# The dt projection of a Mamba and experts layer contracts over 64 rows instead of 16, the added rows being zero

## The chip, the cores and the metric

The kernel runs on one core of a Trainium2 chip. The metric is the device time of one execution, in microseconds (us), the lower the better. Weights are laid out on the host before the launch; the times are of the launch alone.

## The reference

The input x has 32 batches of 512 tokens of width 256, all float32. One layer is computed: a layer norm, a Mamba block, an MLP, a layer norm, and then a mixture of eight experts of which each token takes two, with one shared expert, and a last layer norm. What matters here is the part of the Mamba block between its projections and its scan:

```python
dbc = xc @ x_proj_w.T                       # 512 channels -> 16 + 16 + 16
dt, Bm, Cm = jnp.split(dbc, [16, 32], axis=-1)
dt = jax.nn.softplus(dt @ dt_proj_w.T + dt_proj_b)   # 16 -> 512 channels
def step(h, inp):                            # over the 512 tokens
    dA = jnp.exp(dt_t[..., None] * A)
    h = dA * h + (dt_t * x_t)[..., None] * B_t[:, None, :]
    y = jnp.einsum('bdn,bn->bd', h, C_t)
```

The dt projection, dt @ dt_proj_w.T, contracts over only 16 values for each token. It is the one matmul that the change touches.

## The kernel before, in words

Channels lie on the 128 partitions, tokens along the free axis, so one batch of the 512 inner channels is four tiles of 128x512. All matmuls on the way are float32; each appears in the profile as two MATMUL records (and two LDWEIGHTS).

Each engine runs one list of instructions whose order is fixed when the kernel is built. It is woven from strands: `scan`, `turn` and `weigh` (the state scans, the transposes of their results, and the sum over states), `pre` (everything that leads to the scan of a batch), `post` (everything behind it), and `inputs`, `experts`, `results`, `finish`. The function `weave` merges the strands by a table of places, in which one batch is 64 ticks long; `pre` of a batch runs at negative places, so beside the scans of the batch before it. The tables are the same in both kernels. In steady state, work of three batches is interleaved: the scans of one, the preparation of the next, and the MLP and routing of the one before. Between two engines there are only semaphores; each `wait_ge` stands in front of one instruction and holds back all that is queued behind it on that engine.

The steady work of a batch b:
- ScalarE makes exp(dt*A) for each of 64 (state, tile) pairs into the two banks `psA` (line 755); GpSimdE multiplies dtx by a spread row of B into `dBx` (line 600); VectorE runs the scan into `hs` (line 1231); TensorE transposes `hs` into the banks `psH` (line 977); VectorE adds the transposed state, weighted by C, into `acc` (line 1247).
- TensorE's `pre` for the next batch: transposes of x (line 933), the input projection (942), then the x projection (950), which contracts 128 rows four times and gives 48 rows of output; ScalarE copies those 48 rows to the tile `dbc` (728); four transposes of its C rows (957); and then the dt projection (966): for each of the four channel tiles j, one matmul of 16 rows, with 128 columns of weights and 512 of tokens. All four, for every batch but the first, write to one PSUM bank, `psP`. ScalarE reads the bank twice, for Abs (738) and Relu (741), and matmul j waits for Relu j-1 (`s_dt_relu`).
- Between those four matmuls TensorE's list holds transposes of the running scans (977) and the z projection of `post` (994).
- The expert pairs (1115, 1133, 1148) and the MLP (1040, 1057) fill other places.

The tile `few`, 128 partitions of 1024 floats, holds several small things one above another. Partitions 0 to 15 of its first 512 columns are `w_dt`, the weights of the dt projection, loaded once. Partitions 0 to 47 of the last 512 columns are `dbc`: 16 rows of dt, 16 of B, 16 of C. Partition 64 has small tables for routing, and partition 96 the bias `b2`. Before the change nothing writes partitions 16 to 63 of the weights' columns, nor partitions 48 to 63 of `dbc`'s.

SyncE's list begins with the loads of the weights (line 385), one after another in a fixed order, `dt_proj_w` sixth. VectorE's list begins with small memsets of tables (1195 to 1200) and then waits for all weights. The functions that the diff touches:

Of the kernel before, what the change touches and what calls it, by code (L numbers as in the profile page):

```python
# [116 lines left out]
def build(nc, a, out):  # L117
# [4 lines left out]
    P = 128  # L122
    NB, T, D = a["x"].shape
    DI = a["conv_w"].shape[1] * P
# [4 lines left out]
    R = a["dt_proj_w"].shape[0]  # L129
# [52 lines left out]
    with ctx:  # L182
        def sb(name, shape, dtype=F32):
            return ctx.enter_context(nc.sbuf_tensor(name, shape, dtype))

        def sem(name):
            return ctx.enter_context(nc.semaphore("s_" + name))
# [52 lines left out]

        few = sb("few", [P, DI + T])
        M0, B2 = 64, 96
        w_dt, dbc = few[0:R, 0:DI], few[0:NX, DI:DI + T]
        b2 = few[B2:B2 + 1, 0:D]
        taken, table = 0, []
        for n in (NE * (CAP // P), NT, NE, NE, NE, NT * NE, NT, NT):
# [54 lines left out]
        s_B_in = [sem(f"B_in{i}") for i in range(NBB)]  # L301

        s_zeroed, s_consts, s_halved, s_A_exp = sem("zeroed"), sem("consts"), sem("halved"), sem("A_exp")

        s_bn_post, s_mean_post = sem("bn_post"), sem("mean_post")
        s_tap, s_scan, s_weighed = sem("tap"), sem("scan"), sem("weighed")
# [39 lines left out]
        def per_batch(b, j, n):  # L346
            return b * n + j + 1
# [23 lines left out]
        def bank(b, j):  # L371

            return psP if b else (psP, psE, psG[0], psG[1])[j]
# [8 lines left out]
        @block.sync  # L382
        def _(sp):
            for dst, key_ in loads:
                sp.dma_start(dst if key_ == "dt_proj_w" else dst[:], a[key_]).then_inc(s_weights, 16)
            sp.dma_start(b2, a["mlp_b2"]).then_inc(s_weights, 16)
            sp.dma_start(w_shared[:], a["experts"][NE]).then_inc(s_weights, 16)
# [528 lines left out]
        def _(pe):  # L916
# [5 lines left out]
            def pre():  # L922
                for b in range(NB):
                    xn, c = xnT[b % 2], xc[b % 2]
                    for k in range(KD):
                        yield b
                        pe.wait_ge(s_norm_pre, (b + 1) * NTB)
                        if k:
                            pe.wait_ge(s_xnT, per_batch(b, k - 1, KD))
                        elif b:  # L930
                            pe.wait_ge(s_dt_relu, b * CT)
                        for t in range(NTB):
                            i = pe.transpose(psP[:, t * P:(t + 1) * P], tok_pre[b % 2][:, t, k * P:(k + 1) * P],
                                             ident[:])
                        i.then_inc(s_xn_turned, 1)
                    for j in range(CT):
                        yield b
                        pe.wait_ge(s_xnT, (b + 1) * KD)
                        if b and j:
                            pe.wait_ge(s_tap, per_batch(b, j - 1, CT) * (NK - 1))  # L940
                        for k in range(KD):
                            i = pe.matmul(bank(b, j)[:], w_in[:, k, j * P:(j + 1) * P], xn[:, k, :], start=(k == 0),  # L942
                                          stop=(k == KD - 1))
                            if k == 0:
                                yield b
                        i.then_inc(s_in_mm, 1)
                    yield b
                    pe.wait_ge(s_silu_x, b + 1)
                    for k in range(CT):
                        i = pe.matmul(psP[0:NX, :], w_x[:, k, :], c[:, k, :], start=(k == 0), stop=(k == CT - 1))  # L950
                        if k < CT - 1:
                            yield b
                    i.then_inc(s_x_mm, 1)
                    yield b
                    pe.wait_ge(s_dbc, b + 1)
                    for t in range(NTB):
                        i = pe.transpose(psP[:, t * NS:(t + 1) * NS], dbc[R + NS:NX, t * P:(t + 1) * P],
                                         ident[R + NS:NX, R + NS:NX])
                    i.then_inc(s_C_turned, 1)
                    for j in range(CT):  # L960
                        yield b
                        if j == 0:
                            pe.wait_ge(s_C_tok, b + 1)
                        elif b:
                            pe.wait_ge(s_dt_relu, per_batch(b, j - 1, CT))
                        pe.matmul(bank(b, j)[:], w_dt[:, j * P:(j + 1) * P], dbc[0:R, :], start=True, stop=True).then_inc(  # L966
                            s_dt_mm, 1)

            def turn():
# [182 lines left out]
            def last():  # L1152

                for s_ in range(NLAST + 2):
                    for q, step in ((s_ - 2, 2), (s_ - 1, 1), (s_, 0)):
# [27 lines left out]
                        else:  # L1183
# [4 lines left out]
                            i.then_inc(s_down_last, 1)  # L1188

            weave((turn(), AT["PE_turn"]), (pre(), AT["PE_pre"]), (post(), AT["PE_post"]), (inputs(), AT["PE_inputs"]),  # L1190
                  (experts(), AT["PE_experts"]), (results(), AT["PE_results"]), (last(), AT["PE_last"]))

        @block.vector
        def _(dve):
            dve.memset(where[0], 0).then_inc(s_consts, 1)
            dve.memset(where[1], 0).then_inc(s_consts, 1)
            for k in range(CAP // P):
# [279 lines left out]
```

## Time and profile before

| what | us |
|---|---|
| median of 3 runs | 5192.72 |
| lowest and highest | 5188.47, 5199.28 |
| the profiled execution, its own time | 5198.2 |
| span of the profile | 5196.5 |
| busy: VectorE, TensorE, GpSimdE, ScalarE | 4352.5, 4253.3, 3589.0, 3527.3 |
| mean granted TensorE clock | 0.912 of full |

A busy share is an average over the whole span. The granted clock of TensorE is given as a share of its full speed, 2.4 GHz; the records know only the two values 1.00 and 0.50 (1.2 GHz), and a stretch that holds some of both shows a number between. The batches are counted from 0; batch 10 means the stretch that begins with its first dt matmul.

### The profile page before, as it was taken

The numbers are of one execution on the slowest core, as the hardware profiler recorded it, in microseconds if no ns is written. First come the engines' busy times: TensorE is split into PE (matmuls) and PEld (weight loads), VectorE is DVE, ScalarE is ACT, GpSimd is POOL, SyncE is SP. The second block draws the span as 40 slices with busy tenths as digits, with TensorE's granted clock in tenths as the row PEclk, the third lists the DMA queues.
The fourth block names the chain that finished last, engine by engine and source line by source line (L and its number), as shares of the span: only waits on it lengthen the run. The fifth ranks groups of instructions, "written<-read, shape, count | busy, mean of one in ns | idle before, by whom it ended". The sixth has DMA issues, their size and how long they took to land. (4 is left out here: it accounts for less than half of the span.)

```text
span 5196.5 us, 75832 instructions
## 1 busy us (share of the span) xinstructions
PE 4253.3 (82%) x20928; PEld 2925.9 (56%) x20928; DVE 4352.5 (84%) x6184; ACT 3527.3 (68%) x6433; POOL 3589.0 (69%) x2252
## 2 busy tenths in 40 slices
PE   3788888788888888888888888888888888988882
PEld 2455555565555556555555655555565656655662
DVE  4889899888898898889889888988888888888741
ACT  4666666677766667776776777777677676776642
POOL 4666666666666567777777777777787776787754
PEclk7889899899999999999999999999999889998986
DMA  5122222243333333333333333333344442554555
GB/s 136 54 80 84 84 84 76 74 134 125 112 115 121 108 93 111 100 99 96 96 92 86 105 114 96 96 98 92 84 136 115 121 125 86 165 148 131 161 148 156
DMA packets 357157, 563.53 MB, mean 108 GB/s; under 512 B 40434, under 2 KB 203379, under 8 KB 356611
## 3 DMA queue, kind: packets, MB, share of 16 engines
q1 hardware_dynamic: 286082, 457.85, 28.9%
q0 software_dynamic: 49152, 67.27, 6.3%
q10 hardware_dynamic: 21504, 33.56, 1.7%
q8 instruction: 174, 2.85, 0.2%
q14 instruction: 245, 2.00, 0.1%
HBM read 440.66 MB, written 186.05 MB: 121 GB/s over the span
## 5 line engine op out<-in xcount | busy, mean ns | idle before, releaser
L600 POOL TENSOR_TENSOR dBx<-dtx,Bbc 128x1024 f32<-128x1024 f32 x1024 | 2451.4, 2418 | 684.1 <-DVE hs L1231 632.4
L1231 DVE TENSOR_TENSOR_SCAN hs<-ps,dBx 128x512 f32<-128x512 f32 x2048 | 2409.9, 1207 | 267.9 <-ACT ps L755 91.5
L755 ACT ACTIVATE ps<-dt,A 128x512 f32<-128x512 f32 x2048 | 1393.6, 690 | 610.3 <-DVE hs L1231 596.3
L977 PE MATMUL ps<-ident,hs 128*128 128x128 f32 x8192 | 1323.7, 297 | 461.7 <-DVE acc L1247 296.1
L977 PEld LDWEIGHTS ps<-ident,hs 128*128 128x128 f32 x8192 | 1007.6, 151 | 1018.1 <-DVE acc L1247 519.0
L1247 DVE SCALAR_TENSOR_TENSOR acc<-ps,C_tok,acc 128x512 f32<-128x512 f32 x1792 | 1281.4, 736 | 213.6 <-PE ps L977 193.2
L657 POOL DMA_INDIRECT fx<-Y_slots,slots x256 | 405.5, 1584 | 133.3 <-issue 55.3
L633 POOL DMA_INDIRECT X_slots<-xs,slots x256 | 254.8, 995 | 320.6 <-DVE slots L1358 254.1
L942 PE MATMUL ps<-xnT,w_in 128*128 128x512 f32 x512 | 298.5, 701 | 55.2 <-DVE xc L1220 54.2
L1133 PE MATMUL ps<-xsT,wx 128*128 128x128 f32 x2432 | 322.6, 281 | 23.7 <-ACT xsT L845 23.6
L994 PE MATMUL ps<-xnT,w_in 128*128 128x512 f32 x512 | 340.8, 764 | 0.0
L1133 PEld LDWEIGHTS ps<-xsT,wx 128*128 128x128 f32 x2432 | 301.1, 196 | 41.7 <-issue 40.4
L1220 DVE SCALAR_TENSOR_TENSOR xc<-ps,conv_w,xc 128x511 f32<-128x511 f32 (+2 forms) x384 | 285.3, 744 | 44.5 <-ACT xc L719 36.0
L1040 PE MATMUL ps<-mT,w_m 128*128 128x512 f32 x512 | 239.3, 600 | 26.3 <-ACT mT L801 20.6
L584 POOL TENSOR_TENSOR dt<-dt,dtx 128x1024 f32<-128x1024 f32 x64 | 152.5, 2383 | 141.0 <-ACT dtx L746 141.0
L1024 PE MATMUL ps<-w_out,xc 128*128 128x256 f32 x1024 | 248.0, 379 | 0.0
L1057 PE MATMUL ps<-w_m,post_tmp 128*128 128x256 f32 x1024 | 246.8, 379 | 0.0
L966 PE MATMUL ps<-few 16*128 16x512 f32 x256 | 180.3, 792 | 51.7 <-ACT dt L741 51.4
L719 ACT ACTIVATE xc<-ps,conv_b,conv_w 128x512 f32<-128x512 f32 x128 | 99.3, 776 | 176.8 <-PE ps L942 174.3
L861 ACT ACTIVATE xin<-ps,xin 128x256 f32<-128x256 f32 x304 | 133.0, 468 | 109.7 <-PE ps L1148 109.7
L1057 PEld LDWEIGHTS ps<-w_m,post_tmp 128*128 128x128 f32 x1024 | 191.7, 190 | 25.3
L1024 PEld LDWEIGHTS ps<-w_out,xc 128*128 128x128 f32 x1024 | 191.7, 190 | 24.5
(209 smaller groups left out, 6023.4 us busy)
## 6 DMA issues: line engine op xcount, KB each, us to landing
Bbc<-B_scratch SPq DMA_DIRECT2D x512, 256.0 KB, 3.7
wx<-in_experts SPq DMA_DIRECT2D x308, 384.0 KB, 3.9
Y_slots<-zeros SPq DMA_DIRECT2D x228, 256.0 KB, 4.4
xin<-X_slots SPq DMA_DIRECT2D x308, 128.5 KB, 3.3
Y_slots<-xin SPq DMA_DIRECT2D x308, 128.0 KB, 1.7
xt<-in_x SPq DMA_DIRECT2D x32, 512.0 KB, 4.0
shared<-xt ACTq DMA_DIRECT2D x32, 512.0 KB, 2.6
fx<-shared SPq DMA_DIRECT2D x32, 512.0 KB, 3.6
```

The source lines that it names most:

```text
L600: pool.tensor_tensor(dBx[u % 3][:], dtx[b % 2][:, 2 * h:2 * h + 2, :], Bbc[g % NBB][:, n % CH:n % CH + 1, :].broadcast_to([P, 2, T]), ALU. ...
L657: pool.indirect_dma_start(out=fx[:, t, :], out_offset=None, in_=Y_slots[g % 2], in_offset=bass.IndirectOffsetOnAxis(ap=slots[:, f % NKEPT, ...
L755: act.activation(psA[s % 2][:], dt[b % 2][:, j, :], ACT.Exp, scale=A[:, j, n:n + 1]).then_inc(s_dA, 1)
L942: i = pe.matmul(bank(b, j)[:], w_in[:, k, j * P:(j + 1) * P], xn[:, k, :], start=(k == 0), stop=(k == KD - 1))
L977: i = pe.transpose(psH[w % 2][:, j * P:(j + 1) * P], hs[(n * CT + j) % NHB][:, t * P:(t + 1) * P], ident[:])
L994: i = pe.matmul(psG[j % 2][:], w_in[:, k, DI + j * P:DI + (j + 1) * P], xn[:, k, :], start=(k == 0), stop=(k == KD - 1))
L1024: i = pe.matmul(psG[q][:, t * D:(t + 1) * D], c[:, k, (2 * q + t) * P:(2 * q + t + 1) * P], w_out[:, k, :], start=False, stop=(k == CT - 1))
L1057: i = pe.matmul(psG[q][:, t * D:(t + 1) * D], post_tmp[:, k, (2 * q + t) * P:(2 * q + t + 1) * P], w_m2[:, k, :], start=False, stop=(k == ...
L1133: i = pe.matmul(psE[:, o * HALF + m * P:o * HALF + (m + 1) * P], w[:, m, (2 * k + o) * P:(2 * k + o + 1) * P], xsT[:, (m * KD + k) * P:(m ...
L1220: dve.scalar_tensor_tensor(out=c[:, j, s:], in0=bank(b, j)[:, 0:T - s], scalar=conv_w[:, j, NK - 1 - s:NK - s], in1=c[:, j, s:], op0=ALU.m ...
L1231: dve.tensor_tensor_scan(hs[s % NHB][:], psA[s % 2][:], dBx[s // 2 % 3][:, s % 2, :], 0.0, ALU.mult, ALU.add).then_inc(s_scan, 1)
L1247: dve.scalar_tensor_tensor(out=o, in0=psH[w % 2][:], scalar=C_tok[b % 2][:, t, n:n + 1], in1=o, op0=ALU.mult, op1=ALU.add).then_inc(s_weig ...
```

## The change

The dt projection reads 64 partitions of `few` on both sides instead of 16. Of the weights, rows 16 to 63 are zero, so the B and C rows that now stream through the array beside dt are multiplied by zero, and so are the 16 rows below them, which are zero too. For this, one VectorE memset at the very start clears partitions 0 to 63 of the whole tile `few`, and the load of `dt_proj_w` on SyncE waits for it by a new semaphore.

```diff
         w_dt, dbc = few[0:R, 0:DI], few[0:NX, DI:DI + T]
+        M_DT = 64
+        w_dt0, dbc0 = few[0:M_DT, 0:DI], few[0:M_DT, DI:DI + T]
...
+        s_few = sem("few")
...
             for dst, key_ in loads:
+                if key_ == "dt_proj_w":
+                    sp.wait_ge(s_few, 1)
                 sp.dma_start(dst if key_ == "dt_proj_w" else dst[:], a[key_]).then_inc(s_weights, 16)
...
-                        pe.matmul(bank(b, j)[:], w_dt[:, j * P:(j + 1) * P], dbc[0:R, :], start=True, stop=True).then_inc(
+                        pe.matmul(bank(b, j)[:], w_dt0[:, j * P:(j + 1) * P], dbc0, start=True, stop=True).then_inc(
                             s_dt_mm, 1)
...
         def _(dve):
+            dve.memset(few[0:M_DT, :], 0.0).then_inc(s_few, 1)
             dve.memset(where[0], 0).then_inc(s_consts, 1)
```

## Rows read from the trace of the kernel before

**Rows 1.** Page: busy time by engine, and granted clock in 40 slices.

```profile
PE 4253.3 (82%) x20928; PEld 2925.9 (56%) x20928; DVE 4352.5 (84%) x6184; ACT 3527.3 (68%) x6433; POOL 3589.0 (69%) x2252
PEclk7889899899999999999999999999999889998986
```

**Rows 2.** Windows, one batch each: stretch, length, busy time by engine, clock, DMA share.

```profile
1489.70:1639.90 150.20, 129.95 (x655) 89.22 (x654) 133.63 (x187) 104.25 (x181) 97.48 (x58) 0.94 0.37 120
3313.30:3463.00 149.70, 126.97 (x657) 86.86 (x655) 133.38 (x187) 109.56 (x201) 112.04 (x70) 0.97 0.35 101
1040.30:1189.30 149.00, 126.33 (x655) 86.95 (x654) 133.36 (x187) 104.50 (x182) 97.36 (x58) 0.97 0.42 132
```

**Rows 3.** Waits: engine, tile and line, whom it waited for, us, times, longest.

```profile
DVE acc L1247 <- PE ps L977: 193.2, 201, 2.9
```

**Rows 4.** One line each: instructions, duration in ns (min/median/max), first and last start.

```profile
L966 PE MATMUL ps<-few x256: 587/692/1217, 50.6 to 4785.0; 16*128 16x512 f32 x128
L942 PE MATMUL ps<-xnT,w_in x512: 592/592/1223, 27.5 to 4751.2; 128*128 128x512 f32 x171
```

**Rows 5.** Timeline of PE, batch 10, dt projection: start, us, instruction, idle before it.

```profile
1489.72 1.12 PE L966 MATMUL ps<-few 16*128 16x512 f32 x2
1492.19 2.07 PE L966 MATMUL ps<-few 16*128 16x512 f32 x2 [1.36 <-ACT dt L741]
...
1498.65 1.18 PE L966 MATMUL ps<-few 16*128 16x512 f32 x2
1499.76 1.13 PE L994 MATMUL ps<-xnT,w_in 128*128 128x512 f32 x2
1501.18 1.12 PE L966 MATMUL ps<-few 16*128 16x512 f32 x2 [0.30 <-ACT dt L741]
...
1503.14 1.92 PE L994 MATMUL ps<-xnT,w_in 128*128 128x512 f32 x2
```

**Rows 6.** Timeline of PE, batch 22, the same instructions.

```profile
3321.93 1.12 PE L966 MATMUL ps<-few 16*128 16x512 f32 x2
3322.99 1.13 PE L994 MATMUL ps<-xnT,w_in 128*128 128x512 f32 x2
3324.41 1.12 PE L966 MATMUL ps<-few 16*128 16x512 f32 x2 [0.30 <-ACT dt L741]
...
3325.95 1.02 PE L994 MATMUL ps<-xnT,w_in 128*128 128x512 f32 x2
```

**Rows 7.** Windows of 20 us from the first dt matmul, batches 10 and 22.

```profile
1489.70:1509.70 20.00, 17.58 (x52) 8.93 (x52) 15.84 (x19) 13.06 (x20) 11.54 (x6) 0.74 0.31 107
3313.30:3333.30 20.00, 17.59 (x69) 9.50 (x68) 17.84 (x21) 14.94 (x22) 12.07 (x6) 0.83 0.32 98
```

**Rows 8.** Windows late in the dt projection, batches 2, 31, 22.

```profile
327.90:331.90 4.00, 4.00 (x13) 2.09 (x12) 1.88 (x2) 2.39 (x5) 1.40 (x1) 0.57 0.17 54
4784.90:4788.90 4.00, 4.00 (x13) 2.23 (x12) 1.88 (x2) 2.93 (x6) 3.69 (x3) 0.62 1.06 275
3325.20:3329.20 4.00, 3.95 (x21) 2.33 (x20) 3.04 (x4) 3.15 (x6) 1.36 (x1) 1.00 0.21 50
```

**Rows 9.** Windows with the clock full: x projection (48 columns), and a thinner stretch.

```profile
1632.00:1637.60 5.60, 4.77 (x16) 1.44 (x14) 5.60 (x7) 4.19 (x7) 4.79 (x4) 1.00 0.28 97
1605.10:1610.10 5.00, 3.43 (x24) 2.75 (x24) 4.97 (x7) 4.84 (x10) 3.88 (x3) 1.00 0.01 2
```

**Rows 10.** Windows late in batches 7 and 8.

```profile
1165.30:1170.30 5.00, 3.12 (x6) 1.16 (x7) 3.73 (x13) 0.00 (x0) 0.00 (x0) 0.74 0.94 294
1309.30:1314.30 5.00, 5.00 (x22) 3.26 (x21) 4.90 (x10) 3.33 (x7) 3.83 (x2) 0.68 0.00 0
```

**Rows 11.** Timeline of the start, all engines.

```profile
1.27 0.54 POOL L547 MEMSET xin<- 128x514 f32 x1
...
3.15 0.43 SPq L385 DMA_DIRECT2D few<-in_dt_proj_w  x1
...
13.80 0.29 DVE L1202 TENSOR_SCALAR w_shared<-w_shared 128x256 f32<-128x256 f32 x1 [10.15 <-DMA w_shared<-in_experts]
```

## The prediction

> **What bounds the kernel now.** I read the page first: VectorE is busy 84% of the span and TensorE 82%, and the clock row shows TensorE below full clock somewhere in nearly every slice [rows 1]. Neither engine is full, so the question is who waits for whom, and where. One batch as a window gives 150.2 us, 133.6 of them with VectorE busy [rows 2]: 16.6 us of a batch is all that a faster TensorE could ever give, and most of that belongs to other engines and places. The list of waits names the place that matters here: VectorE's weighted sum (line 1247) waits 193.2 us in all for TensorE's transposes (line 977) [rows 3].
>
> The timeline of TensorE around the dt projection shows when that happens. In batch 10 the first dt pair takes 1.12 us, the second 2.07 [rows 5]; at full clock a pair of 512 columns takes 1.02 us (the z projection in [rows 6]). So the clock has fallen to 1.2 GHz right behind the first dt matmul. It comes back by the third (1.18), and falls again right behind the fourth: the z projection that starts at 1503.14 takes 1.92 us. What the engine did before that second fall is telling. From 1498.65 to 1503.1 it was never idle for more than 0.30 us, yet two of its three 512-column matmuls there were the dt matmuls of 16 rows [rows 5]. Elsewhere the clock stays at 1.00 over a thinner stretch, 3.43 us busy of 5.0, that has no 16-row matmul in it, and also over one of 4.77 us of 5.6 in which the x projection does most of the work, with 48 columns of weights but all 128 rows [rows 9]. Busy time alone doesn't tell these apart and the weights' columns don't either; the rows that stream do.
>
> The two falls differ in what they cost. Batch 22 has the first fall but not the second (its z projection at 3325.95 takes 1.02 us [rows 6]). Over 20 us from the first dt matmul, batch 10 has 15.84 us of VectorE work and a clock of 0.74, batch 22 has 17.84 and 0.83 [rows 7]: VectorE's list is the same there, so the second fall costs VectorE 2.0 us.
>
> **The change part by part.**
>
> *The matmul itself.* 128 dt matmuls (256 records) with 64 rows instead of 16. The trace has none of 64 rows; the nearest rows on both sides are 16 rows, 587 ns at least and 692 in the median, and 128 rows, 592 ns in both [rows 4]. The rows don't change how long 512 columns stream; the 100 ns between the median of the one and the other go, at most, if it no longer pays what a 16-row matmul pays behind a 128-row one: 256 x 0.1 = 26 us of TensorE's time won at best, and as much lost if 64 rows paid double. Neither lies on the path, since VectorE and ScalarE set the pace there. I take 0.
>
> *The second fall.* It stands behind the fourth dt matmul in 21 of the 32 batches: batches 2, 4, 8 to 15, 17 to 19, 21, 23 to 28 and 31, of which [rows 8] shows the first, the last, and one without it (0.57 and 0.62 against 1.00, VectorE 1.88 against 3.04 us of 4.0). Before it the array is busy nearly without a gap, so four times the rows in two of three matmuls should keep the clock. How much of the 2.0 us lasts to the end of the batch can be read from batches that lack the fall: batch 7 takes 149.0 and batch 22 149.7 us, against 150.2 for batch 10 [rows 2], so 1.2 and 0.5 us are kept. The rest is given back at the end of the batch, where another fall meets the input projection: batch 7 has 0.74 and VectorE busy only 3.73 of 5.0 us there, while in batch 8 it comes 6 us earlier, in a stretch where VectorE loses nothing (4.90 of 5.0) [rows 10]. I take 1.2, batch 7's, as its expert work is the same as batch 10's. 21 x 1.2 = 25 us; with 0.5 it would be 10, with all of the 2.0, 42.
>
> *The first fall.* All 32 batches have it, from about 1492 to 1498.6 in batch 10, some 7 us. In front of it TensorE does one dt matmul, a few transposes and then waits 1.36 us for Relu [rows 5]. More rows can't fill that idle time. Even in batch 22, which has this fall alone, VectorE is idle only 20 - 17.84 = 2.16 us in the 20 [rows 7]; if the first fall went too, up to 32 x 2.16 = 69 us would follow. I take 0 here, because idle time stands in front of the fall, and keep 69 as the far end.
>
> *The start.* The memset of 64x1024 is bounded by GpSimdE's 128x514 in 0.54 us: about twice that, 1.1 us [rows 11]. SyncE reaches the load of `dt_proj_w` at 3.15 us, and VectorE's next work after its tables waits until 13.80 for the last weights. So the new wait finds the semaphore already set, with eleven loads queued behind it that would otherwise slip; and VectorE's 1.1 us lies under 10.15 us of idle time. 0; without that cover 1.1 us once.
>
> Sum: 0 - 25 + 0 + 0. Against the profiled execution's own 5198.2 us that is 5173; this execution lay 5.5 above the median of 5192.7, so 5168.
>
> **The rivals.**
>
> *No change (5193).* The clock would heed only whether TensorE is busy, and 16 rows would be as good as 128. For it: a fall also stands behind idle time, as in the first fall, and the second one could be its echo, since TensorE has just come back from 1.2 GHz. Against it: the nearly gapless stretch in front of the second fall beside the thinner one that keeps its clock [rows 5, 9]. It also covers the case that rows with zero weights don't count. The Trainium skill, "TensorE: Matmul & The Clock Gate", Part 1, says that the clock gate is set "based on how busy the PE has been recently" and says nothing of rows; by that rule this kernel's time would stay at 5193, and [rows 9] against [rows 5] speak against it.
>
> *Both falls go (5130).* If 64 rows count enough to carry even the thin stretch, TensorE arrives at the third dt matmul some 3 us earlier, half of the 7 us spent at half the clock. Priced at half of the far end above, 35 us, on top of the 25: 5133, and some luck at the end of the batch makes 5130. For it: the stretch ahead holds transposes of 128 rows beside the dt matmul. Against: 1.36 us idle.
>
> *Slower (5212).* The order of work is fixed, and where a fall lands depends on when the batch arrives. A batch shorter by 1 or 2 us shifts all later falls; if the shift holds the late one steadily in the input projection, where it takes 5.0 - 3.73 = 1.27 us from VectorE in batch 7 [rows 10], and an additional one in that place takes as much again, 30 batches lose 2.5 us each = 76, less the full local gain of 21 x 2.0 = 42 and the part of the loss that batches already pay, some 15: about 19 us slower. It decides if less than 1.3 us of the local gain is left over per batch. Against it: batches 7 and 22 had exactly this and were still shorter.
>
> **How the numbers follow.** Forecast 0.58, no change 0.18, both falls 0.16, slower 0.08. The forecast's own range goes from 5150 (all of the 2.0 kept) to 5185. The whole range takes in both falls at 5115 (nearly the far end of 69 us) and, above, no change: 5115 to 5193. What a measurement can tell from no change is about 0.2%, 10 us. Within the forecast, about one part in eight lies inside that. Faster: 0.51 + 0.16 + a little of the rest = 0.70; same: 0.07 + 0.15 = 0.22; slower 0.08.
>
> **What would show it.** Right: in the profile of the changed kernel the clock over the first 20 us of batches 8 to 15 is 0.83 or more instead of 0.74 and VectorE has about 17.8 us of work there; the z projection behind the fourth dt matmul takes 1.02 us; the mean clock rises from 0.912 to about 0.925; VectorE's wait for line 977 drops from 193 us by some 30 to 40; batches last 149 us. The dt records themselves stay at 587 to 692 ns. Wrong: the fourth dt matmul is still followed by a pair of 1.92 us (then rows don't count, or not enough), or the falls go and the batches still last 150.2 us, which would mean that the gain is given back before the batch ends.

## The result

The changed kernel takes 5133.1 us (median of 4 runs, 5114.8 to 5143.9) against 5190.6 us of the kernel before, run beside it. The ratio is 0.988, 95% interval 0.985 to 0.992. That is 57 us faster, where 25 were forecast. It lies inside the whole range (5115 to 5193) but outside the forecast's own, 5150 to 5185, and at the time of the rival "both falls go" (5130). Repeated on two different chips, it gave 0.988 (0.986 to 0.990) and 0.990 (0.987 to 0.992). The profiled execution took 5135.8 us with a span of 5134.1 and a mean granted clock of 0.930 (0.912 before). The added lines shift the numbers: line 385 is now 390, 741 is 746, 966 is 971, 977 is 982, 994 is 999, 1231 is 1237, 1247 is 1253; in the experiments an added matmul shifts them by one or two more.

The page of the changed kernel, the lines that answer to [rows 1]:

```profile
PE 4166.5 (81%) x20928; PEld 2875.0 (56%) x20928; DVE 4350.4 (85%) x6185; ACT 3522.6 (69%) x6433; POOL 3586.6 (70%) x2252
PEclk6999999899999999999999999999999899999986
```

VectorE's work is what it was (4352.5 before). TensorE's busy time fell by 87 us though it streams the same columns: it is the same work at a higher clock. From the list of waits, how long VectorE's weighted sum waits for TensorE's transposes; it was 193.2 us in [rows 3]:

```profile
DVE acc L1253 <- PE ps L982: 155.5, 188, 2.9
```

The dt matmul itself, answering to [rows 4] (duration in ns, min/median/max): 587/692/1217 became

```profile
L971 PE MATMUL ps<-few x256: 589/693/1219, 50.7 to 4724.4; 64*128 64x512 f32 x128
```

So 64 rows take as long as 16 did, to within 2 ns. Over 20 us from the first dt matmul, batches 10 and 14 of the changed kernel (length, busy time of PE, PEld, DVE, ACT and POOL, clock, DMA share and GB/s), for [rows 7]:

```profile
1474.70:1494.70 20.00, 17.58 (x66) 9.49 (x66) 17.23 (x20) 14.85 (x22) 11.80 (x5) 0.83 0.32 108
2073.30:2093.30 20.00, 16.48 (x79) 9.28 (x78) 19.48 (x23) 16.82 (x24) 12.22 (x7) 1.00 0.36 116
```

The two lines are the two main kinds of batch that the changed kernel has. Batch 10 has lost the second fall and kept the first, and looks as batch 22 did before: 0.83, and 17.23 us of VectorE's work, against 0.74 and 15.84 in batch 10 before. Batch 14 has lost both: over these 20 us the clock is at 1.00 throughout, and VectorE is busy 19.48 of 20 us. TensorE's timeline in batch 10, for [rows 5]:

```profile
1477.14 1.98 PE L971 MATMUL ps<-few 64*128 64x512 f32 x2 [1.36 <-ACT dt L746]
1479.06 1.97 PE L982 MATMUL ps<-ident,hs 128*128 128x128 f32 x8
1480.82 1.91 PE L999 MATMUL ps<-xnT,w_in 128*128 128x512 f32 x2
...
1484.84 1.12 PE L999 MATMUL ps<-xnT,w_in 128*128 128x512 f32 x2
1486.26 1.12 PE L971 MATMUL ps<-few 64*128 64x512 f32 x2 [0.30 <-ACT dt L746]
...
1487.81 1.02 PE L999 MATMUL ps<-xnT,w_in 128*128 128x512 f32 x2
```

The second dt pair still takes 1.98 us and the transposes and the z projection behind it 1.97 and 1.91, so the first fall is there. The z projection behind the fourth dt matmul, 1.92 us in [rows 5], takes 1.02 at 1487.81. The same work in batch 14, with the idle time in front of the second dt matmul unchanged at 1.36 us:

```profile
2073.32 1.12 PE L971 MATMUL ps<-few 64*128 64x512 f32 x2
2075.80 1.12 PE L971 MATMUL ps<-few 64*128 64x512 f32 x2 [1.36 <-ACT dt L746]
2076.86 1.09 PE L982 MATMUL ps<-ident,hs 128*128 128x128 f32 x8
2077.78 1.02 PE L999 MATMUL ps<-xnT,w_in 128*128 128x512 f32 x2
```

All at 2.4 GHz: 1.12, 1.09 and 1.02 us.

I counted the falls in the profiles, over batches 1 to 31. A batch has the first fall if the clock is at 1.2 GHz for more than 1 us between its first and third dt matmul, and the second if it is for more than 1 us between 9.6 and 16.5 us from the first (batches 16 and 20 of the kernel before have a longer first fall and no second).

| kernel | first fall, of 31 | second fall | us at 1.2 GHz in the whole profile |
|---|---|---|---|
| before, 16 rows | 31 | 21 | 921 |
| changed, 64 rows, profiled three times | 17, 20, 17 | 2, 2, 0 | 720, 705, 720 |

The two batches under second fall in the first two profiles, 26 and 28, have one fall there instead of two (in batch 26 it begins 9.0 us in), and the count has them among those that lost the first. So the second fall is gone as forecast, and by this count the first went too in 11 to 14 of 31 batches, which was not.

The count ends 16.5 us into the batch, and the falls behind it changed as well. In the kernel before, each of the 18 batches from 7 to 29 that has the second fall has a third, 20 to 37 us in; in the changed kernel batch 10 has lost it, while batch 14 has one at a new place. Stretches from 25 to 35 us behind the first dt matmul, batch 10 before, batch 10 changed, batch 14 changed:

```profile
1514.70:1524.70 10.00, 7.94 (x32) 4.58 (x31) 8.42 (x11) 8.17 (x20) 9.71 (x5) 0.83 0.25 79
```

```profile
1499.70:1509.70 10.00, 6.61 (x35) 4.42 (x36) 9.70 (x14) 8.44 (x18) 9.79 (x6) 1.00 0.28 91
2098.30:2108.30 10.00, 9.18 (x37) 5.58 (x38) 9.65 (x12) 8.21 (x15) 9.92 (x6) 0.83 0.40 119
```

Batch 14's new fall costs VectorE next to nothing there (9.65 us of work against 9.70).

Whole batches, for [rows 2] (batches 10, 13 and 19):

```profile
1474.70:1624.90 150.20, 128.15 (x656) 88.04 (x655) 133.70 (x187) 103.98 (x182) 97.51 (x57) 0.95 0.38 120
1926.20:2073.30 147.10, 124.47 (x655) 85.66 (x654) 133.04 (x187) 109.72 (x202) 111.86 (x69) 0.99 0.39 113
2823.20:2969.90 146.70, 124.46 (x655) 85.55 (x654) 132.93 (x187) 109.95 (x202) 111.77 (x69) 0.99 0.40 113
```

Batch 10 lasts 150.2 us, exactly as before, though its second fall is gone. Batches 13 and 19 had both falls and lasted 153.0 and 153.1 us; without either they last 147.1 and 146.7.

### The profile page after: what moved, and what is told of

Its sections match the earlier page's. It is cut to its first block and busy times, and to the rows that moved or that the text cites. A ratio compares the mean times of both kernels' runs of the same rounds, so it can differ in the third digit from the quotient of the medians.

```text
span 5134.1 us, 75833 instructions
## 1 busy us (share of the span) xinstructions
PE 4166.5 (81%) x20928; PEld 2875.0 (56%) x20928; DVE 4350.4 (85%) x6185; ACT 3522.6 (69%) x6433; POOL 3586.6 (70%) x2252
## 5 line engine op out<-in xcount | busy, mean ns | idle before, releaser
L982 PE MATMUL ps<-ident,hs 128*128 128x128 f32 x8192 | 1295.6, 292 | 486.6 <-DVE acc L1253 284.5
L982 PEld LDWEIGHTS ps<-ident,hs 128*128 128x128 f32 x8192 | 975.9, 148 | 1013.9 <-DVE acc L1253 527.5
L947 PE MATMUL ps<-xnT,w_in 128*128 128x512 f32 x512 | 292.5, 688 | 57.3 <-DVE xc L1226 56.1
L999 PE MATMUL ps<-xnT,w_in 128*128 128x512 f32 x512 | 299.8, 679 | 0.0
L589 POOL TENSOR_TENSOR dt<-dt,dtx 128x1024 f32<-128x1024 f32 x64 | 153.0, 2391 | 132.2 <-ACT dtx L751 132.2
L971 PE MATMUL ps<-few 64*128 64x512 f32 x256 | 163.5, 724 | 51.1 <-ACT dt L746 50.7
```

The costliest lines, as they stand in the source:

```text
L982: i = pe.transpose(psH[w % 2][:, j * P:(j + 1) * P], hs[(n * CT + j) % NHB][:, t * P:(t + 1) * P], ident[:])
L999: i = pe.matmul(psG[j % 2][:], w_in[:, k, DI + j * P:DI + (j + 1) * P], xn[:, k, :], start=(k == 0), stop=(k == KD - 1))
```

## The experiments

All times are medians beside runs of the kernel before on the same chip, three jobs in all; the kernel before had 5192.4, 5198.8 and 5196.6 us in them. The theory was that the clock of TensorE follows the rows that stream through the array and not its busy time alone (A). The main rival was that rows don't matter and the change only moved the work against the falls, or that busy time is all that counts (B).

**The memset and the wait alone, 16 rows.**

```diff
-        M_DT = 64
+        M_DT = 16
```

(The diff here and in the two runs after it is against the changed kernel; the memset still clears 64 rows.) 

> The changed kernel's memset and wait at the start are kept, but the dt matmul reads 16 rows as before. Theory A: no gain, 5185 to 5200 us, the second fall of the clock back in about 21 of 32 batches. Rival B (the new start shifts the whole program against the clock's falls): 5115 to 5145 us, as with 64 rows.

Measured: 5194.2 us, ratio 1.000 (0.998 to 1.001). First fall in 31 batches, second in 21. Batch 10 over the 20 us:

```profile
1488.00:1508.00 20.00, 17.58 (x52) 8.94 (x52) 15.80 (x19) 13.06 (x20) 11.51 (x6) 0.74 0.30 107
```

The line is that of the kernel before (0.74, 15.80 against 15.84). The start of the program and its new semaphore cost nothing and gain nothing. That part of B is out.

**32 and 48 rows.** The cut is that of 32 rows; the other run has 48 in its place.

```diff
-        M_DT = 64
+        M_DT = 32
```

> 32 rows in the dt matmul, the rest as in the changed kernel. Theory A1 (each row counts): the busy stretch of the third and fourth dt matmul keeps its clock, the thin one of the first two doesn't: 5155 to 5175 us, first fall in all 32 batches, second in none or few. Theory A2 (rows count in groups of 32, of which 16 rows fill one already): no gain, 5185 to 5200 us. If 32 rows do all that 64 do: 5130 us.

> 48 rows, which are exactly the rows that hold data (dt, B and C); no row of zeros streams. Theory A1 (each row counts): between 32 and 64 rows, 5140 to 5170 us; the first fall, which 64 rows take away in 13 of 32 batches, stays in more of them. Theory A2 (groups of 32, two of them filled): the same as 64 rows, 5115 to 5145 us.

Measured: 32 rows 5163.4 us, ratio 0.995 (0.994 to 0.997); 48 rows 5156.1 us, 0.994 (0.991 to 0.996). In the same job the changed kernel itself:

> The changed kernel again, 64 rows, for a firm number beside the others. Theory A (the clock heeds how many rows stream through the array, so the dt matmuls now hold it up): 5115 to 5145 us. Rival B (the gain came from something else, such as where the falls of the clock happened to land): the same, this run doesn't tell them apart.

Measured: 5128.7 us, 0.988 (0.986 to 0.990).

| rows in the dt matmul | us | first fall | second fall | us at 1.2 GHz |
|---|---|---|---|---|
| 16 | 5194.2 | 31 | 21 | 891 |
| 32 | 5163.4 | 31 | 6 | 787 |
| 48 | 5156.1 | 31 | 0 | 757 |
| 64 | 5128.7 | 20 | 2 | 705 |

32 rows, batches 10 and 14 over 20 us, the one without and the other with the second fall:

```profile
1487.70:1507.70 20.00, 17.58 (x66) 9.56 (x66) 17.40 (x20) 14.56 (x21) 12.02 (x6) 0.83 0.30 109
2088.70:2108.70 20.00, 17.59 (x52) 8.79 (x52) 15.92 (x19) 13.12 (x20) 11.64 (x6) 0.74 0.27 95
```

48 rows, batch 10:

```profile
1491.50:1511.50 20.00, 17.58 (x65) 9.52 (x65) 17.26 (x20) 14.89 (x22) 11.80 (x5) 0.83 0.33 108
```

The ladder settles three things. 32 rows already do more than 16, so rows don't count in full groups of 32 (A2 is out for this step). The second fall goes between 16 and 48 rows, the first only between 48 and 64, and in part. (With the second goes the third: of batches 7 to 29, 18 have it with 16 rows and none with 48.) And the step from 48 to 64 adds nothing but zeros, in the weights and in the data, and yet brings 27 us: for the clock, rows of zeros do.

**More busy time, no more rows.** Each dt matmul of the kernel before is issued twice.

```diff
+                        pe.matmul(bank(b, j)[:], w_dt[:, j * P:(j + 1) * P], dbc[0:R, :], start=True, stop=True)
                         pe.matmul(bank(b, j)[:], w_dt[:, j * P:(j + 1) * P], dbc[0:R, :], start=True, stop=True).then_inc(
                             s_dt_mm, 1)
```

> The kernel before, with each dt matmul of 16 rows issued twice into the same bank (the second one's result stands): TensorE is busier by 0.86 us at each of the four places, without more rows at a time. Theory A (rows that stream count): both falls of the clock stay, in 31 and some 15 to 25 batches, and the time is 5190 to 5215 us. Rival B (busy time counts, rows don't): the falls go as with 64 rows and more, 5120 to 5160 us.

Measured: 5423.5 us, ratio 1.043 (1.040 to 1.045). TensorE's timeline of batch 9, lines 966 and 967 being the two dt matmuls:

```profile
1412.63 2.07 PE L966 MATMUL ps<-few 16*128 16x512 f32 x2 [1.36 <-ACT dt L741]
1414.50 1.91 PE L967 MATMUL ps<-few 16*128 16x512 f32 x2
1416.34 1.97 PE L978 MATMUL ps<-ident,hs 128*128 128x128 f32 x8
...
1420.80 2.07 PE L966 MATMUL ps<-few 16*128 16x512 f32 x2
1422.66 1.91 PE L967 MATMUL ps<-few 16*128 16x512 f32 x2
1424.50 2.08 PE L995 MATMUL ps<-xnT,w_in 128*128 128x512 f32 x2
1426.51 2.07 PE L966 MATMUL ps<-few 16*128 16x512 f32 x2
1428.38 1.91 PE L967 MATMUL ps<-few 16*128 16x512 f32 x2
...
1432.83 1.91 PE L978 MATMUL ps<-ident,hs 128*128 128x128 f32 x8
...
1437.29 1.02 PE L995 MATMUL ps<-xnT,w_in 128*128 128x512 f32 x2
```

From 1414.50 to the end of the dt matmuls the timeline shows no idle time of TensorE, and every pair of dt takes 1.9 to 2.1 us, so the clock stays at 1.2 GHz. It is back at 2.4 only behind some 6 us in which nothing but matmuls of 128 rows streamed (1.02 us at 1437.29). The 20 us from the first dt matmul:

```profile
1410.30:1430.30 20.00, 18.64 (x32) 7.20 (x31) 9.66 (x11) 8.72 (x14) 8.97 (x4) 0.53 0.31 108
```

0.53, and VectorE has 9.66 us of work in 20. The expectation was right in the sign and far too low in the price: 225 us more than the kernel before beside it (5198.8), where 5215, 16 more, was the most expected. I had priced the falls as if they kept their length; they grew: in batch 9 the clock is at 1.2 GHz for 24 us without a break. Nor had I priced the added matmuls. All dt matmuls together keep TensorE busy for 387 us instead of 180, much of it at half the clock and in a place where the engine has no idle time; how much of the 225 us is theirs and how much comes from the longer falls, no run separates. Rival B, that busy time is what counts, is out.

**One added matmul in front of the first dt matmul.** The first fall stays in 17 to 20 batches. If rows are what the stretch in front of it lacks, a matmul of 128 rows there should help.

```diff
+                        if j == 0:
+                            pe.matmul(psP[:, 0:256], ident[:], xn[:, 0, 0:256], start=True, stop=True)
                         pe.matmul(bank(b, j)[:], w_dt0[:, j * P:(j + 1) * P], dbc0, start=True, stop=True).then_inc(
```

> The changed kernel (64 rows) with one more matmul in front of the first dt matmul of each batch: identity by 256 columns of the normed input, 128 rows, into the bank that the dt matmul then overwrites, 0.43 us at full clock. Theory A: this is what the thin stretch lacks in the 17 to 20 batches where the first fall stays; it then stays in under 8, and the time is 5085 to 5120 us. If the first fall is worth nothing where it stays: 5129 us and up to 14 more (32 times 0.43).

Measured: 5119.9 us, ratio 0.985 (0.982 to 0.987). First fall in 14 batches, 624 us at 1.2 GHz. Its timeline in batch 10, where the changed kernel had the fall (line 972 is the added matmul):

```profile
1478.56 0.60 PE L972 MATMUL ps<-xnT,ident 128*128 128x256 f32 x2
1479.09 1.12 PE L973 MATMUL ps<-few 64*128 64x512 f32 x2
1481.56 1.12 PE L973 MATMUL ps<-few 64*128 64x512 f32 x2 [1.36 <-ACT dt L746]
...
1483.55 1.02 PE L1001 MATMUL ps<-xnT,w_in 128*128 128x512 f32 x2
```

Repeated on another chip:

> 64 rows with the added matmul of 128 rows and 256 columns in front of the first dt matmul, again. If its lead over the changed kernel is real, a ratio of about 0.985 to the kernel before (5115 to 5125 us); if it was the draw of that job, 0.988.

> The changed kernel (64 rows) once more, on the same chip as the three variants that go beyond it. 5115 to 5145 us, a ratio of 0.988 to the kernel before.

Measured: 5116.7 us, 0.985 (0.983 to 0.987), against 5135.3 us, 0.990 (0.987 to 0.992), for the changed kernel on the same chip. So the added matmul, useless as arithmetic, wins another 19 us. The intervals of the ratios just touch, but each of its six runs (5107.5 to 5120.3) is faster than each of the six of the changed kernel (5122.6 to 5157.6), and the first job gave the same 0.985. This is the fastest version that was run. It removed fewer falls than expected (14 and 13 left, not under 8), but it halved most that it left: 13 of the 14 and 11 of the 13 last about half as long as the usual first fall, of the changed kernel's 17 to 20 only 2 to 4. In the first 9.6 us of batches 1 to 31 the clock is at 1.2 GHz for 53 and 55 us in sum, against 114 to 124 in the changed kernel. This, more than the count, goes with the 19 us.

The same added matmul with 16 rows:

```diff
+                        if j == 0:
+                            pe.matmul(psP[:, 0:256], w_dt[:, 0:P], dbc[0:R, 0:256], start=True, stop=True)
```

> As the run before, but the added matmul has 16 rows instead of 128: the same 0.43 us of TensorE, an eighth of the rows. Theory A: the first fall stays in 15 to 22 batches as without it, 5125 to 5145 us. Rival B (busy time counts): the same as with the added matmul of 128 rows.

Measured: 5168.3 us, 0.994 (0.991 to 0.996). First fall in 28 of 31 batches. Batch 10 over 20 us with 16 rows in the added matmul, and then with 128:

```profile
1506.80:1526.80 20.00, 17.59 (x67) 9.55 (x66) 16.94 (x20) 14.72 (x21) 11.82 (x5) 0.83 0.33 110
```

```profile
1479.10:1499.10 20.00, 16.44 (x79) 9.26 (x78) 19.04 (x23) 16.86 (x24) 12.03 (x6) 1.00 0.38 135
```

0.83 against 1.00, and 16.94 against 19.04 us of VectorE's work, for nearly the same time on TensorE (0.69 us the pair with 16 rows, 0.60 with 128): 48 us between the two kernels. It gains 31 us over the kernel before beside it, where 64 rows with nothing added gain 57 to 64 in the other jobs: it is 27 to 33 us slower than those, where at most 16 were expected. The 16-row matmul doesn't only fail to help, it also brings falls that weren't there; why was not tried further.

The added matmul without the change:

> The kernel before (16 rows) with the added matmul of 128 rows and 256 columns in front of the first dt matmul of each batch. Theory A: the first fall goes in some 5 to 12 of the batches, the second stays in 15 or more: 5165 to 5190 us. If what the added matmul does were independent of the dt matmul's rows, it would gain here what it gains over the kernel with 64 rows.

Measured: 5195.5 us, 0.999 (0.998 to 1.000); first fall in 25 batches, second in 19. Some falls went, as expected (850 us at 1.2 GHz against 891 with 16 rows in the ladder), but the time didn't follow: 5165 to 5190 us were expected. Where it was lost was not traced; that the added matmul costs as much as it gains is not shown. Together with the 64 rows it is worth more than alone.

More of the same:

> As fill64 with 512 columns in the added matmul, 0.86 us instead of 0.43. Theory A: the first fall, left in 14 of 31 batches by 256 columns, is left in 5 or fewer; each is worth at most some 2 us and the longer matmul costs 0.43 us in each batch that didn't need it, so 5105 to 5130 us. If the falls that are left don't depend on what stands in front of the first dt matmul, still about 14 of them and 5120 to 5140 us.

> As fill64, with the same added matmul also in front of the second dt matmul of each batch but the first. It stands behind the wait for Relu, so behind the idle time. If the falls that 256 columns leave begin only behind the second dt matmul, they go too: 5 or fewer batches with the first fall, 5100 to 5125 us. If they are set before it, the second added matmul only costs: 5120 to 5140 us, as many falls as fill64.

The first puts 512 columns into the added matmul; the second adds one also in front of the second dt matmul:

```diff
-                        if j == 0:
+                        if j < 2 and (b or j == 0):
```

Measured: 5136.9 us, 0.989 (0.986 to 0.992), and 5131.5 us, 0.988 (0.985 to 0.991). First falls 19 and 20. Both expectations on the falls were wrong: no fewer were left than with one matmul of 256 columns. Batch 14, without falls there, with the longer matmul, over 20 us:

```profile
2076.10:2096.10 20.00, 16.41 (x79) 9.23 (x78) 18.61 (x22) 16.89 (x24) 11.82 (x6) 1.00 0.36 117
```

VectorE has 18.61 us of work in it where the shorter one left 19.04 (batch 10 above; both numbers recur to 0.1 us in the other batches from 9 to 24 whose clock is full over the 20 us, and with nothing added it is 19.4 to 19.5). So each 0.43 us of added matmul takes 0.43 us from VectorE here. Why falls remain that this doesn't reach is open. In the batches that keep them they mostly begin elsewhere, 3.3 to 4.5 us behind the first dt matmul, where batches 8 to 11 of the changed kernel have 1.8 to 2.6; I ran nothing that holds that place fixed.

## Why the prediction was right, and where its sizes were off

**In short.** The mechanism held: more rows keep the clock, and the second fall goes. The sum did not: 25 us were forecast and 57 to 64 measured, because the first fall, a term taken at 0, also went in part, and because the second was priced too low. That the time still lies in the range is owed to the far end kept for "both falls go", to which 0.16 was given; the forecast's own 5150 to 5185 missed it.

**What bounds the kernel** held. That VectorE idles in this place because TensorE's low clock makes its transposes late is shown by VectorE's 19.48 us of work in 20 as soon as the clock is full.

**The matmul's own time**, taken as 0: right, 589/693 ns against 587/692.

**The start**, taken as 0: right, both by the run with 16 rows and by its rows, where the memset ends at 2.00 (it takes 0.91 us, 1.1 were estimated) and SyncE comes to the load at 3.18, 3.15 before:

```profile
1.09 0.91 DVE L1200 MEMSET few<- 64x1024 f32 x1 [1.09 <-PEq L1474]
...
3.18 0.43 SPq L390 DMA_DIRECT2D few<-in_dt_proj_w  x1
```

**The second fall** was the one that was priced, at 21 x 1.2 = 25 us. The mechanism is shown: it is gone with 48 rows, which leave the first fall in all 31 batches, so that kernel measures this term, with the third fall that goes with it: 5194.2 - 5156.1 = 38 us, 1.8 for each of 21. The local price of 2.0 us was too high, as batch 22 is not batch 10: in batch 10 itself VectorE wins 1.4 us over the 20 (15.84 to 17.23). The share that lasts was too low. But it isn't a share of each batch. In batch 10 nothing was kept: over its last 40 us, kernel before and then changed,

```profile
1599.70:1639.90 40.20, 32.14 (x164) 20.85 (x162) 38.60 (x75) 24.84 (x41) 26.00 (x20) 0.96 0.29 99
```

```profile
1584.70:1624.90 40.20, 32.29 (x157) 20.38 (x155) 37.09 (x70) 23.55 (x39) 25.85 (x19) 0.92 0.28 93
```

VectorE lost 1.5 us (38.60 against 37.09) at a clock of 0.92 instead of 0.96, about what it had won in the 20 us. Batches 9 and 12 kept nothing either. Others kept more than the fall itself had cost: batch 11, which also lost only the second, went from 149.9 to 147.0, and batch 24, which lost half of its first fall besides, from 157.6 to 153.1. The later falls move with the batch, some into and some out of places where they hurt. Two batches that happened to lack the fall (7 and 22) were too few to price it by.

**The first fall** is where the sum was mis-sized. The prediction said "More rows can't fill that idle time" and took 0. They don't fill it, but the rows that stream beside it count: with 64 rows the first fall is left in 17 to 20 batches, and the step from 48 to 64 rows, which changes nothing else, brings 27 us. 38 + 27 = 65 us (by construction the difference between 16 and 64 rows in that job), against 57 to 64 under the kernel before in the three jobs. The case stood among the rivals as "both falls go", at 5130 and a chance of 0.16; what came was that case for two batches in five, with a time at the rival's. The starts of the first dt matmuls in the two traces price the falls batch by batch: of batches 0 to 30, six lost only the first fall and are 1.9 us shorter each, 13 lost only the second and are 1.6 shorter each, and five lost both and are 4.4 shorter each; the other seven, 26 and 28 with them, give 3.8 us in sum. The far end of 2.16 us for a first fall was thus near the mark; what failed is the reason for the 0, that idle time in front of the fall decides.

**The signs.** Most came as named: 1.02 us behind the fourth dt matmul, VectorE's wait down by 38 us (30 to 40 expected), a mean clock of 0.930 (0.925). Two did not. Batches 12 and 15 have 0.77 and 16.4 us of VectorE's work, under the 0.83 and 17.8 named for batches 8 to 15, as one long fall begins ahead of their first dt matmul; and batches 9 and 10 still last 150.2 us, which stood as a sign of being wrong. In those batches the gain is indeed given back, over the program it is not.

**No change** is refuted, and with it the part that rows with zero weights don't count. The Trainium skill, "TensorE: Matmul & The Clock Gate", in its table "Why this matters for your kernels", advises to keep TensorE busy continuously to get to full clock. The run with doubled matmuls of 16 rows kept it busy from 1414.50 to the end of the dt matmuls at 1430.2 and stayed at 1.2 GHz, so that trace does not agree with the page for matmuls of few rows; behind matmuls of 128 rows alone the clock came back.

**Slower** didn't come, but its mechanism, gains given back by falls that move, is real, as batch 10 shows. It cost part of the gain over the program and never all.

## What to carry to other kernels

When a matmul contracts over few rows and the clock falls around it, look in the timeline for a TensorE that is busy and yet slow; filling the contraction with rows of zeros cost next to nothing in its time here (587 against 589 ns) and can keep the clock, if the partitions are free and hold finite numbers. Price such a change by a ladder (16, 32, 48, 64 rows) and not by the few batches that lack a fall by chance, because a gain at one place moves all later falls. More busy work of few rows is the wrong cure: it made this kernel 225 us slower.

## What the hardware showed that was not expected

- Rows of zeros count for the clock: 48 to 64 rows added only zeros on both sides, and the first fall was gone from 11 of 31 batches.
- A TensorE without a gap stayed at 1.2 GHz: in the run with doubled 16-row matmuls the mean over the 20 us was 0.53, and 0.893 over the program.
- A matmul of 128 rows whose result is thrown away made the program 19 us faster, one of 16 rows in the same place made it 27 to 33 us slower (each against the kernel before of its own job; in one job 48 us lie between the two).
